# Expert tiles: the second layer's bias moved from TensorE products to a broadcast row on VectorE, the high columns' scaling to ScalarE

## What is computed

```python
x = x + gelu(x @ mlp_w1 + mlp_b1) @ mlp_w2 + mlp_b2
xm = _ln(x, ln2_g, ln2_b)
...
for e in range(NEXP):
    he = gelu(xm @ exp_w1[e] + exp_b1[e])
    oe = he @ exp_w2[e] + exp_b2[e]
    moe_out = moe_out + comb[..., e:e + 1] * oe
return x + moe_out
```

## Time and profile before

| | |
|---|---|
| median of three runs | 1374.36 us (1368.64 to 1376.65) |
| the profiled execution | 1368.88 us |
| its span | 1367.1 us |
| TensorE matmuls | 1236.9 us, 90% of the span |
| TensorE weight loads | 1043.0 us, 76% |
| VectorE | 986.1 us, 72% |
| ScalarE | 666.7 us, 49% |
| GpSimd | 411.9 us, 30% |
| mean granted clock of TensorE | 0.972 |
| DMA | 123.32 MB, mean 90 GB/s |

### The profile page before, as it was taken

The page is one execution under the profiler, slowest core; times in us unless marked ns, Lnnn a source line. Parts: engine busy times, 40 slices in busy tenths (PEclk is TensorE's granted clock), DMA queues, the critical chain, the costliest instruction groups (busy, mean ns, idle before and its releaser), DMA issues.

```text
span 1367.1 us, 28240 instructions
## 1 busy us (share of the span) xinstructions
PE 1236.9 (90%) x9938; PEld 1043.0 (76%) x9938; DVE 986.1 (72%) x2685; ACT 666.7 (49%) x1520; POOL 411.9 (30%) x395
## 2 busy tenths in 40 slices
PE   4589999999999999999986899999898999999996
PEld 3367777777677776777765699998787998998995
DVE  3367777777777867778665678777777878888884
ACT  0154555545555455654556555554533444544531
POOL 1111111110111101111010027877776344344344
PEclk7699999999999999999997899999999999999998
DMA  2092211122101222012400333436566666666652
GB/s 92 21 250 59 62 53 40 28 60 60 53 28 39 60 60 53 20 48 60 96 10 9 151 85 73 81 82 176 126 157 159 145 179 155 146 179 154 149 119 30
DMA packets 93596, 123.32 MB, mean 90 GB/s; under 512 B 9152, under 2 KB 85801, under 8 KB 89554
## 3 DMA queue, kind: packets, MB, share of 16 engines
q1 hardware_dynamic: 69090, 100.75, 24.7%
q0 software_dynamic: 24432, 21.62, 11.5%
HBM read 68.94 MB, written 53.38 MB: 89 GB/s over the span
## 4 chain that ended last, share of the span: by engine, by line
PE 59%; DVE 16%; issue 12%; POOL 7%; ACT 3%; another core or an unknown queue 1%; DMA 1%; POOLq 0%; DVEq 0%; SPq 0%; ACTq 0%
PE PS L1486 51%; PE PS L1489 8%; POOL expert_rows L690 3%; POOL rs L624 2%; DVE st L1010 2%; DVE XA L1021 1%; DVE nb L1086 1%; DVE mv L1013 1%; DVE Z L1021 1%; DVE H L1053 1%; ACT XAT L744 1%; POOL out L678 1%; DVE ZS L1068 1%; DVE H L1050 1%
## 5 line engine op out<-in xcount | busy, mean ns | idle before, releaser
L1486 PE MATMUL PS<-w2r,GH 128*120 (+1 forms) x864 | 262.8, 362 | 1.7 <-DVE GL L1255 1.1
L925 ACT ACTIVATE GF<-PS,b1c 128x480 f32<-128x480 f32 x216 | 142.4, 660 | 249.6 <-PE PS L1486 230.0
L624 POOL TENSOR_TENSOR rs<-ve,minus_half 128x3 f32<-128x3 f32 (+1 forms) x80 | 58.8, 736 | 624.6 <-DVE ve L1015 624.6
L728 POOL DMA_INDIRECT out<-YO,ids x100 | 163.0, 1630 | 184.2 <-DVE flag L1439 158.1
L1486 PE MATMUL PS<-w2r,GL 128*120 (+1 forms) x864 | 216.9, 251 | 0.0
L766 ACT ACTIVATE PX<-PS,nb 128x165 f32<-128x165 f32 x576 | 176.9, 413 | 66.2 <-DVE nb L1086 57.7
L1486 PE MATMUL PS<-XH,w1r 128*128 128x480 f32 x432 | 171.7, 398 | 13.3 <-ACT GF L925 8.1
L1486 PEld LDWEIGHTS PS<-w2r,GH 128*120 128x120 f32 x864 | 156.9, 182 | 4.9 <-DVE GL L1255 4.2
L1486 PEld LDWEIGHTS PS<-w2r,GL 128*120 128x120 f32 x864 | 159.1, 184 | 0.0
L1489 PE MATMUL PS<-ident,PX 128*128 128x128 f32 x864 | 138.6, 289 | 19.7 <-DVE PT L1091 11.7
L1086 DVE TENSOR_REDUCE nb<-PS 128x6 f32<-128x990 f32 x96 | 113.4, 1183 | 50.8 <-PE PS L1486 50.4
(11 more groups left out here) (249 smaller groups left out, 2312.4 us busy)
## 6 DMA issues: line engine op xcount, KB each, us to landing
w1r<-expert_w_parts SPq DMA_DIRECT2D x25, 1536.0 KB
expert_rows<-empty SPq DMA_DIRECT2D x45, 369.4 KB, 6.0
RT<-expert_rows SPq DMA_DIRECT2D x25, 369.4 KB
X<-x_scratch SPq DMA_DIRECT2D x11, 360.0 KB, 6.2
out<-X POOLq DMA_DIRECT2D x11, 360.0 KB, 5.7
XP<-in_patches SPq DMA_DIRECT2D x32, 108.0 KB
H<-in_txt SPq DMA_DIRECT2D x16, 192.0 KB, 3.9
out<-H SPq DMA_DIRECT2D x16, 192.0 KB
```

What stands on the lines that cost most here:

```text
L624: nc.gpsimd.tensor_tensor(rs[:, k - 1, 0:n], ve[:, k - 1, 0:n], eps_half[:, 0:n], ALU.pow).then_inc(rstd_ready[k - 1], 1)
L728: nc.gpsimd.indirect_dma_start(out[:, :], bass.IndirectOffsetOnAxis(ap=ids[:, i, t:t + 1], axis=0), YO[:, i % 2, t, :], None, bounds_check ...
L925: nc.scalar.activation(GF[:, m % 3, :], PS[:, 2 + m % 2, 0:GT], ACT.Gelu, bias=bias, scale=1.0).then_inc(gelu_ready, 1)
L1486: return nc.tensor.matmul(o, l, r, start=start, stop=stop)
```

## The change

The expert's bias row is no longer added by a product with `ones`. Instead SyncE loads the row `exp_b2[e]`, repeated on 120 partitions, into a new tile `b2t` with two places (`load_b2`). ScalarE multiplies the high columns of the bank by the gate weight into `YO` (`row_high_out`, after `row_high` in its turn). VectorE adds the other 192 columns times the weight, and then `b2t` times the weight. The dense pair's bias stays a product, so `b2r` shrinks to that one row. The loop of SyncE gets a wait for `y_ready` ahead of each `load_b2`, at its end.

```diff
-    b2r = sb(two, "b2r", [P, NF, D], F32R)
+    b2r = sb(two, "b2r", [P, D], F32R)
+    b2t = sb(two, "b2t", [TB, 2, D])
...
+        def load_b2(i, at):
+            e = sp.value_load(plan[0:1, 0, i:i + 1], min_val=0, max_val=NE - 1)
+            sp.dma_start(b2t[:, at, :], a["exp_b2"][bass.ds(e, 1), :].rearrange("o d -> (o d)").partition_broadcast(TB)).then_inc(b2_in[at], 16)
...
         for i in range(2):
             load_tile(i, i)
             load_w1(i, i)
+            load_b2(i, i)
...
             load_tile(i, i % 2)
             sp.wait_ge(up_ps, (GROUPS + i - 1) * KH)
             load_w1(i, i % 2)
+            sp.wait_ge(y_ready, (i - 1) * TG)
+            load_b2(i, i % 2)
...
             if i >= 0 and i + 2 < TILES:
                 row_high(i + 2)
+            if i >= 0:
+                row_high_out(i)
+
+        def row_high_out(i):
+
+            at, q = i % 2, i // 2
+            act.wait_ge(meta_ready, i + 1)
+            if q > 0:
+                act.wait_ge(added[at], 16 * TG * q)
+            for t in range(TG):
+                act.wait_ge(down_ps, (GROUPS + i) * TG + t + 1)
+                nc.scalar.activation(YO[:, at, t, :], PS[0:TB, 4 + t, 0:D], ACT.Copy, scale=cs[:, i, t:t + 1]).then_inc(high_out, 1)
 
         for i in range(-1, TILES - 1):
             turn(i)
+        row_high_out(TILES - 1)
...
-        steps.link(nc.vector.memset(b2r[:, :, :].bitcast(F32), 0.0))
+        steps.link(nc.vector.memset(b2r[:, :].bitcast(F32), 0.0))
         dve.wait_ge(vec_in, NVEC * 16)
-        steps.link(cp(b2r[0:1, :, :], rb2[:, :, :]))
-        tt(b2r[32:33, :, :], rb2[:, :, :], b2r[0:1, :, :].bitcast(F32), ALU.subtract)
+        steps.link(cp(b2r[0:1, :], rb2[:, :]))
+        tt(b2r[32:33, :], rb2[:, :], b2r[0:1, :].bitcast(F32), ALU.subtract)
...
             dve.wait_ge(meta_ready, i + 1)
-            if q > 0:
-                dve.wait_ge(added[at], 16 * TG * q)
+            dve.wait_ge(b2_in[at], 16 * q + 16)
             for t in ts_of:
-                dve.wait_ge(down_ps, (GROUPS + i) * TG + t + 1)
+                dve.wait_ge(high_out, i * TG + t + 1)
                 w = cs[:, i, t:t + 1]
-                steps.link(ts(YO[:, at, t, :], PS[0:TB, 4 + t, 0:D], w, None, ALU.mult))
                 stt(YO[:, at, t, :], PS[0:TB, 4 + t, D:2 * D], w, YO[:, at, t, :], ALU.mult, ALU.add).then_inc(down_read, 1)
                 dve.wait_ge(down_read, (GROUPS + i + 1) * TG + t + 1)
+                steps.link(stt(YO[:, at, t, :], b2t[:, at, :], w, YO[:, at, t, :], ALU.mult, ALU.add))
                 cp(flag[:, t:t + 1], ident[0:TB, 0:1]).then_inc(y_ready, 1)
...
-                    mm(bank[:, 0:D], gl[:, k, TB * t:TB * t + TB], w(k, D), False, False)
+                    last = mm(bank[:, 0:D], gl[:, k, TB * t:TB * t + TB], w(k, D), False, bias is None and k == KH - 1)
...
-                mm(bank[:, 0:D], ones[:, :], bias, False, True).then_inc(down_ps, 1)
+                if bias is not None:
+                    last = mm(bank[:, 0:D], ones[:, :], bias, False, True)
+                last.then_inc(down_ps, 1)
```

## The result

The change makes the kernel slower: 1430.64 us as the median of six runs (1421.36 to 1440.11), against 1375.51 for the kernel before (1368.64 to 1378.67, six runs). The ratio is 1.042, with a 95% interval of 1.0382 to 1.0457. The profiled execution took 1436.2 us, with a span of 1434.5.

The account below looks back on a forecast made before the run. TensorE was taken to bound the expert stage (14.57 us a tile); 1368.9 + 53.2 (19 stalls of 2.8) + 3.0 - 8.4 + 0.4 = 1417.1, moved halfway to the median: 1420 us. Range 1385 to 1455 us.

Parts of the forecast that it names:

- the landing's range: Expert-stage row load, issue to landing: 4.7 us taken, bounds 3.1 and 6.2, giving 1385 to 1449 us.
- The terms of the stall: Before each turn's transposes: 0.80 + 1.36 + 4.7 = 6.9 us against 4.1 available, a stall of 2.8 us.
- The room: Expert stage, from row sums done (1203.1) to transposes wanted (1207.24): 4.1 us for issue and landing of the rows.
- The clock: Rival: each expert-turn stall also halves TensorE's clock, making the beat 18.5 us and the time about 1446; chance 0.18.
- The bias products: Four removed TensorE products per expert tile: 0.38 us a tile, 9.5 us for 25 tiles, counted as 8.4.
- ScalarE's part: ScalarE's scaling per expert tile fills idle time, but makes the row sums 0.6 us later, costless by itself.
- the ring: Stalled transposes delay second layer, row sums and next row load, so the beat becomes 17.0 us and does not recover.
- The ends: Turns 1 and 2 cost 3 us together, turn 3 nothing, the last row sum 0.4 us; bias-tile setup is hidden.
- the faster case: Rival: two SyncE loads issue within 0.8 us and landing takes 3.1, so no stall: 1360 us; chance 0.06.
- The quick landing: Rival: the row load lands in 3.1 us, a 1.2 us stall per turn, 1385 us; chance 0.15.
- the lateness of the row sums alone: Rival: rows come in time, but row sums 0.6 us later eat the 0.38: 1369 to 1372 us; chance 0.04.
- ScalarE's long standstill: Rival: ScalarE's 11.47 us stop at 1029 to 1040 us goes or doubles: 6 us less or 11 more; chance 0.1.

Follow-up runs that it names:

- the second profile: The changed kernel, unchanged, profiled once more: 1430.26 us, with 296.7 us in the 17 steady turns.
- The doubled load: The changed kernel with a second bias load per tile, into a spare tile, behind the first: 1490.78 us, ratio 1.0862.
- the repaired versions: The changed kernel with a later bias load, four places, or the wait ahead of the weights: ratios 0.9987, 0.9951 and 0.9963 to the kernel before.
- the run with the later load: The changed kernel with the bias row of tile i - 2 loaded where that of tile i was: 1369.58 us, ratio 0.9987 to the kernel before.

## Why the prediction was right

**The sign and the mechanism.** The forecast was 1420 us, from 1385 to 1455, and the measured time is 10.6 us above it. The sum itself said 1417.1, and the step halfway to the median happened to point the right way. (That step is in the high end of the landing's range, 1449, but not in the low end; with it that end is 1387 and not 1385.) The forecast came from the order of SyncE's loads, and three runs show that order as the cause: the same wait with four places, with a later load, and ahead of the weights instead of `RT` leaves a beat of 14.20 us.

**The terms of the stall**, in the round shown above: from the last flag to the first issue 0.74 us (forecast 0.80); from one load to the next 1.36 (1.36); from issue to the release of the weight loads 4.85 in the mean of the twenty loads from 1055 us on, 4.19 to 5.69 (4.7). The estimate of 2.9 us was worked out from the Trainium skill's page DMA: Bandwidth & Descriptors, Anatomy of one DMA, whose fit of 2.0 us plus the bytes at 436 GB/s is for transfers issued by GpSimd, while this load is SyncE's; the trace shows none that short, and the measurement decides. The room, measured between the same two marks as in the forecast, is from the last flag at 1262.02 to where the weight loads had nothing left, 1269.31 - 3.15 = 1266.16: 4.1 us (forecast 4.1). The weight loads' wait is 53.0 / 19 = 2.8 us (forecast 2.8); the second profile has 2.7.

**The beat.** Forecast 17.0 us. In the first profile eleven of the turns after rows 7 ran at a mean clock of 0.99 or more, and they average 17.0; the mean of all is 17.44. In the second profile the six turns at 1.00 average 16.8, and all 17.45.

**The clock.** I gave it as a rival of its own, with all turns falling or none. It was a part instead: in 8 of 22 turns of the first profile the mean clock was under 0.95. Over the 17 turns that is about 0.44 x 17 = 7.5 us (11 by the same count in the second profile), the largest term that my sum lacked. The doubled load shows the rival in full.

**The bias products.** 0.38 us a tile forecast, 0.41 measured.

**ScalarE's part.** Free in the steady turns, as forecast; but the 0.6 us of later row sums are inside the ring, where they are not free: they are a part of the 2.8 us. My text counted them there, though it called them costless by themselves.

**The ends.** In the four turns from rows 3 on, my terms make 1.5 us for turn 2, none for turn 3, 2 x 2.8 for turns 4 and 5, less 1.5 for the products: 5.6 us. The two profiles of the changed kernel lie 8.0 and 5.1 us above those of the kernel before, on both sides of it. Turn 3 did hide its stall: the weight loads waited there for 0.7 us in the first profile and not at all in the second. One thing was too small: from the first issue of `RT` to rows 3 the profiles with both the bias load and ScalarE's scaling took 73.2 to 76.4 us, those with one of them or neither 71.8 to 72.9: two us in the mean that I had called hidden. I did not find which step it is. That, and the scatter of the early turns, may be why the repaired versions gain 2 to 8 us instead of the 9 of the products; that is not shown, and how it divides stays open.

**The rivals that fell.** Two loads issued within 0.8 us, on which the faster case rested, do not occur: from the bias load to the load of `RT` it is 1.24 us at the least in the first profile, and mostly 1.36. The quick landing does not occur either. That the lateness of the row sums alone decides is refuted by the run with the later load. ScalarE's long standstill did not come back as it was: in the changed kernel the waits of ScalarE and VectorE with no engine behind them are 4.6 us in total in the first profile and 9.8 in the second, where the kernel before has 16.2 and 17.3.

## What to carry to other kernels

An engine that issues loads in order passes every wait on to all that is queued behind it. So when a load gets a wait, look first for the next load behind it and at when that one is wanted, and only then at the load itself. A bias row of 90 KB that nobody waited for made the kernel 55 us slower, because it stood one place ahead of rows that were wanted 4 us later; a second pair of places, or one place later in the order, gave all of it back. The Trainium skill's rule (DMA: Bandwidth & Descriptors, Rules for kernel authors) is to issue a transfer early and to wait for it late; the runs here show that it has to be kept for all that stands in the queue, not only for the transfer at hand.

If such a delay closes a ring, it does not wear off over the turns but sets the beat; add up the ring and compare it with the beat of the bound engine.

## What the runs showed of the hardware that I had not expected

TensorE's clock fell in some turns and not in others after nearly the same idle time. From the timeline of the changed kernel, three groups of eight transposes, which take 1.04 us at 2.4 GHz and 1.86 at 1.2:

```profile
1077.31 1.86 PE L1511 MATMUL PS<-ident,RT 120*128 120x120 f32 x8 [2.94 <-DMA RT<-expert_rows]
1164.98 1.38 PE L1511 MATMUL PS<-ident,RT 120*128 120x120 f32 x8 [2.06 <-DMA RT<-expert_rows]
1337.87 1.04 PE L1511 MATMUL PS<-ident,RT 120*128 120x120 f32 x8 [3.22 <-DMA RT<-expert_rows]
```

And as a stretch, a turn in which it fell:

```profile
1145.61:1164.98 19.37, 17.32 (x86) 15.58 (x86) 11.82 (x29) 8.32 (x14) 7.05 (x4) 0.84 0.45 115
```

After 2.94 us idle it was at half, after 2.06 us it fell within the group, and after 3.22 us it stayed at full speed. In the second profile 8 of 22 turns fell again, four of them the same turns and four others, with the same total of the 17 turns to 0.3 us. So between 2.1 and 3.2 us of idle time the length of the last pause alone does not decide whether the clock falls; what else does, no run here shows. In the steady turns a fall cost 1.4 to 2.9 us of matmul time (15.8 to 17.3 us a turn where full speed has 14.4). At 3.7 us in the mean (the doubled load) nearly every turn fell, and 1.36 us of SyncE a turn cost 2.96 us of beat (20.40 for 17.44).
